# First metric block beside the normalisation, root of the shift bound on VectorE, and closing work spread wider, in an attention layer with a gated feed-forward

## The chip, the cores and the metric

The kernel runs on one core of a Trainium2 chip. The metric is the device time of one execution in microseconds, lower is better. The kernel before takes 607.02 us, the median of three runs (606.62 to 607.74).

## What is computed

One transformer layer on a single sequence of 2048 tokens with 128 features, in fp32. Both halves are gated residuals on a modulated layer norm; the attention works on a hyperbolic log map and multiplies its queries by a learned metric. Cut to what matters:

```python
h = layernorm(x) * (1 + ca) + sa
v = log_map(mu, project(h))            # sqrt, arccosh, one factor for each token
q, k, vv = v @ Wq.T, v @ Wk.T, v @ Wv.T            # 16 heads of width 8
g = |eta + 0.1 * tanh(tanh((h - mu) @ W1.T + b1) @ W2.T + b2)|   # the metric
at = softmax((q * g) @ k.T / sqrt(8))  # 16 heads, 2048 x 2048
x = x + ga * project(mu + 0.1 * (at @ vv) @ Wo.T)
h = layernorm(x) * (1 + cb) + sb
x = x + gb * (silu(h @ wg.T) * (h @ wu.T)) @ wd.T  # hidden width 384
```

## The kernel before

Tokens are cut into four blocks of 512 queries (`NB`, `BT`) and sixteen key tiles of 128 (`NT`). The program has three parts.

*Opening.* VectorE, ScalarE and GpSimd normalise all tokens, and TensorE transposes them (`metric_T`). ScalarE copies the four transposed blocks out (`copy_hT`), then takes the square roots and the logarithm of the log map (`root`, line 433, and line 448), each on request of VectorE, which scales the result to `v` (line 976). Only behind that come the metric of block 0 (`tanh1`, `metric2`, `tanh2`, lines 422 to 431 and 585), the keys of all four blocks (`k_of`), the queries of block 0 (`q_of`), and the splitting of each into three bf16 parts (`k_split1`, `k_rest`, `k_low`, `q_split1`, `queries_rest`, `queries_low`). The parts go to DRAM and come back with another partition layout (`store_k`, `load_k`, `load_q` on SyncE's queue, in written order). The softmax isn't shifted by the true maximum but by a bound: the largest key norm times the query norm of the head. `nk` and `nq` sum the squares, `k_max` takes the maximum, block by block in one PSUM bank, `bound` takes the square root on ScalarE, and `shift` writes the row that `load_shift` puts beside the queries. The first score matmul waits for that row.

*Four blocks* (`block_steps`). A block has 64 steps (`STEPS`): four groups of four heads, each over 16 key tiles. Step j issues on TensorE the scores of two head pairs (`score(j, 0)` and `score(j, 1)`, line 703, sixteen matmuls in all) and between them the product of step j - 2 with the values (`product`, line 720, eight matmuls). ScalarE takes two exponentials of 128x1024 in a step (line 510). Scores lie in three slots of two PSUM banks each, used in turn (`u % 3`); a score waits until the exponential of the slot's last user is done. The count starts anew with each block; since 128 isn't a multiple of three, the first two scores of a block fall on the slots of the last two exponentials before them, and steps 1 and 63 issue their product ahead of the first score. After 16 steps a group's sums are copied out by VectorE (`evacuate`, line 1100), and the next group's first product waits for it (`o_evac`).

In block 0 the steps also carry the values (`V_AT`) and metric, queries and query norms of blocks 1 to 3, at steps written by hand: `M1_AT`, `M2_AT`, `Q_AT`, `NQ_AT`. All of them, as the closing work later, share one PSUM bank (`M_bank`). `nq(b)` puts a block's query norms there, VectorE copies them away (`queries_norm`, line 1065) and signals `nq_sb`, and `metric1(b + 1, 0)` on TensorE, the next to write the bank, waits for `nq_sb` (line 576). After step 49 (`ROOT_AT`) ScalarE takes the three roots (line 473) together.

In blocks 1 to 3 the steps also carry the closing work of the block before, at `AT_WO`, `AT_TR`, `AT_GATE`, `AT_UP` and `AT_DOWN`: output projection, transpose, three gate and three up matmul groups, and the down projection in four pieces.

*The end.* The closing work of block 3 stands alone.

All engines run their own list in order. TensorE's is one list: a wait in it holds all that stands behind.

Of the kernel before, what the change touches and what calls it, by code (L numbers as in the profile page):

```python
# [24 lines left out]
ALU = mybir.AluOpType  # L25
# [31 lines left out]
AT_WO, AT_TR, AT_GATE, AT_UP, AT_DOWN = 8, 15, (19, 24, 29), (22, 27, 32), (37, 39, 41, 43)  # L57
# [3 lines left out]
M1_AT, M2_AT, Q_AT, NQ_AT, ROOT_AT = ((7, 10), (21, 24), (35, 38)), (13, 27, 41), (16, 30, 44), (19, 33, 47), 49  # L61
# [17 lines left out]
def build(nc, x, columns, wmod, fixed, w1t, w2t, w_att, wgt, wut, wdt, out):  # L79
    with ExitStack() as ctx:  # L80
# [27 lines left out]
        hs_bf = sb("hs_bf", [P, H], BF16)  # L108
# [21 lines left out]
        def tmp(words, *shape, dt=F32):  # L130
# [5 lines left out]
            if len(shape) == 2:  # L136
# [10 lines left out]
        shift_f = [O_sb[0:H, 0, :], O_sb[0:H, 3, :], x_res[0:H, :, :].rearrange("p a b -> p (a b)"),  # L147
                   h_tm[0:H, 0:TPB, :].rearrange("p a b -> p (a b)")]
# [58 lines left out]
        names = """c_in wmod_in w_in hs_ready ffn_in const_ready pe_mod mod_ready silu_ready ffn_ready  # L207
# [21 lines left out]
        def ring(j):  # L229

            return j % RING if j < STEPS - 1 else 1
# [137 lines left out]
        def _(pool):  # L369
            pool.memset(half[:, :], 0.5).then_inc(S["const_ready"], 1)  # L370
            pool.memset(mhalf[:, :], -0.5).then_inc(S["const_ready"], 1)
            pool.memset(V_op[:, :, :], 1.0).then_inc(S["ones_ready"], 1)
            pool.wait_ge(S["const_ready"], 2)
# [13 lines left out]
            pool.tensor_copy(hs_bf[:, :], hs_sb).then_inc(S["hs_ready"], 1)  # L387
# [24 lines left out]
        def _(act):  # L412
# [29 lines left out]
            for b in range(NB):  # L442
                copy_hT(b)
# [4 lines left out]
            act.activation(ln_u, u, ACT.Ln).then_inc(S["ln_out"], 1)  # L448

# [5 lines left out]
            def k_split1(b):  # L455
# [3 lines left out]
                act.activation(k_parts[b][:, 0, :], bank(2 + b % 2), ACT.Identity).then_inc(S["k_hi"], 1)  # L459
                act.activation(sqks[b], bank(2 + b % 2), ACT.Square).then_inc(S["k_sq"], 1)  # L460
# [5 lines left out]
            def bound(b):  # L466

                if b == 0:
                    act.wait_ge(S["nq_ps"], 1)
                    act.wait_ge(S["kmax_ready"], 1)  # L470
                else:
                    act.wait_ge(S["nq_sb"], b)
                act.activation(shift_f[b], bank(6)[0:H, :] if b == 0 else shift_f[b], ACT.Sqrt,
                               scale=kmax[0:H, NB:NB + 1]).then_inc(S["bound"], 1)

            for m in range(MH):
                tanh1(0, m)
            copy_vT(0)
            copy_vT(1)
            k_split1(0)  # L480
            tanh2(0)
            act.wait_ge(S["k_res"], 1)
            act.activation(k_parts[0][:, 1, :], rks[0], ACT.Identity).then_inc(S["k_mid"], 1)
            q_split1()
            k_split1(1)
            act.wait_ge(S["q_res"], 1)
            act.activation(q_parts[0][:, 1, :], rqs[0], ACT.Identity).then_inc(S["q_mid"], 1)
            k_split1(2)
            k_split1(3)
            act.activation(sqq[:, :], g_fm[:, 0, :], ACT.Square).then_inc(S["q_sq"], 1)  # L490
            bound(0)
            act.activation(silu_c[:, 1:2], c_c, ACT.Exp).then_inc(S["exp_table"], 1)

            def later(j):
# [9 lines left out]
            def block_steps(Bk, tails):  # L504
                for j in range(STEPS):
                    for half_ in range(2):
# [3 lines left out]
                        act.activation(probs[:, 2 * ring(j) + half_, :], slot_bank(u % 3), ACT.Exp)\  # L510
# [18 lines left out]
            def blocks(p):  # L529
                block_steps(NB * p, False)  # L530
                with act.Fori(NB * p + 1, NB * (p + 1)) as Bk:
                    block_steps(Bk, True)
# [15 lines left out]
        def _(pe):  # L548
# [41 lines left out]
            for b in range(NB):  # L590
                metric_T(b)
            for m in range(MH):
                metric1(0, m)

# [7 lines left out]
            def k_of(b):  # L602
                pe.wait_ge(*((S["vT_sb"], b + 1) if b < 2 else (S["vT_late"], b - 1)))
                if b >= 2:
                    pe.wait_ge(S["k_sq"], b - 1)
                    pe.wait_ge(S["k_res"], b - 1)
                else:
                    pe.wait_ge(S["m1_sb"], MH)
                pe.matmul(bank(2 + b % 2), wk_sb, vT[:, b, :], start=True, stop=True).then_inc(S["k_ps"], 1)  # L609
# [7 lines left out]
            def nk(b):  # L617
                pe.wait_ge(S["k_sq"], b + 1)
                pe.wait_ge(*((S["nk_done"], b) if b else (S["vT_late"], 1)))
                pe.matmul(bank(0)[0:H, :], hs_bf[:, :], sqks[b], start=True, stop=True).then_inc(S["nk_ps"], 1)  # L620
# [10 lines left out]
            def nq(b):  # L631
                pe.wait_ge(S["q_sq"], b + 1)
                pe.wait_ge(S["q_f"], b + 1)
                pe.matmul((M_bank if b else bank(6))[0:H, :], hs_bf[:, :], sqq[:, :], start=True, stop=True)\
# [7 lines left out]

            v_T(0)
            v_T(1)
            k_of(0)
            metric2(0)
            v_T(2)
            v_T(3)
            q_of(0)
            for b in range(1, NB):  # L650
                k_of(b)
            pe.wait_ge(S["hs_ready"], 1)
            for b in range(NB):
                nk(b)
            nq(0)

# [13 lines left out]

            def keep_warm(n, to):

                for _ in range(n):
                    ins = pe.matmul(to, ones_bf[:, 0:P], ones_bf[:, 0:BT], start=True, stop=True)  # L674
                ins.then_inc(S["warm"], 1)


            def score(Bk, j, p, half_):
# [14 lines left out]
                if u >= 3:  # L693
# [3 lines left out]
                for i in range(2):  # L697
                    h = GH * g + 2 * half_ + i
                    if isinstance(Bk, int):
                        at_q = (Bk % 2) * H * BT + h * BT  # L700
                        for c in range(COLS):
                            at_k = P * (kt % TPB) + CW * c
                            ins = pe.matmul(slot_bank(u % 3)[CW * c:CW * (c + 1), i, :],  # L703
                                            K_op[0:rows, kt // TPB, h, at_k:at_k + CW], Q_op[0:rows, at_q:at_q + BT],
                                            start=True, stop=True, tile_position=(0, CW * c))
                    else:
                        ins = pe.matmul(slot_bank(u % 3)[:, i, :],
# [4 lines left out]
            def product(Bk, j):  # L712
# [5 lines left out]
                for i in range(GH):  # L718
                    h = GH * g + i
                    ins = pe.matmul(O_bank[32 * i:32 * (i + 1), :], V_op[:, kt, VW * h:VW * h + 32],  # L720
                                    probs[:, 2 * ring(j) + i // 2, BT * (i % 2):BT * (i % 2 + 1)],
# [37 lines left out]
            def block_steps(Bk, tails, p):  # L759
                for j in range(STEPS):  # L760
                    early = j in (1, STEPS - 1)
                    if not early:
                        score(Bk, j, p, 0)
                    if j >= 2:
                        product(Bk, j - 2)
                    elif tails:
                        product(Bk - 1, STEPS + j - 2)
                    if early:
# [16 lines left out]
            def blocks(p):  # L785
# [16 lines left out]
                product(last, STEPS - 2)  # L802
                product(last, STEPS - 1)
# [27 lines left out]
            keep_warm(7, M_bank)  # L831
            for done, n in (("vT_late", 2), ("k_sq", NB), ("k_res", NB), ("nk_done", NB), ("bound", 1)):
# [24 lines left out]
        def _(dve):  # L857
# [24 lines left out]
            vec.did(dve.memset(flag_f[:, :], 1.0))  # L882

# [60 lines left out]
            dve.tensor_scalar(a2, n2, 1.0, EPS, ALU.add, ALU.add).then_inc(S["root_in"], 1)  # L944
            dve.wait_ge(S["root_out"], 2)
# [35 lines left out]
            def metric(b):  # L981

                vec.after()
                dve.wait_ge(S["m2_sb"], b + 1)
                vec.did(dve.tensor_scalar(g_fm[:, b, :], g_fm[:, b, :], 0.1 * DH ** -0.5, eta_s, ALU.mult, ALU.add))  # L985

# [19 lines left out]
            def k_max(b):  # L1006
                dve.wait_ge(S["nk_ps"], b + 1)
                dve.tensor_reduce(kmax[0:H, b:b + 1], bank(0)[0:H, :], AX.X, ALU.max).then_inc(S["nk_done"], 1)  # L1008

            def shift(b):  # L1010

                dve.wait_ge(S["bound"], b + 1)
# [3 lines left out]
            vec.did(dve.tensor_scalar(eta_s, eta_c, DH ** -0.5, None, ALU.mult))  # L1016
            def k_rest(b):
                dve.wait_ge(S["k_sq"], b + 1)
# [309 lines left out]
```

## Time and profile before

| | us |
|---|---|
| median of three runs | 607.02 |
| profiled execution, device time | 608.64 |
| its span, first to last instruction | 606.6 |
| outside the span | 2.0 |
| TensorE busy (matmul) | 544.9 |
| ScalarE busy | 524.8 |
| VectorE busy | 152.6 |
| GpSimd busy | 21.5 |

Busy time is the union of the instructions' durations; a matmul's duration contains the depth of the pipeline, so the distance of starts tells more than the busy share. "PEclk" is the granted TensorE clock as a share of full speed: 1.00 is 2.4 GHz, 0.50 is 1.2 GHz. In the timeline, rows of the same instruction that follow one another closely are merged: start, time from the first start to the last end, engine, line, operands, count, and in brackets the idle time before and what ended it. In the chain of waits a piece lasts until the next piece of the path begins.

### The profile page before, as it was taken

To read this page: it belongs to the slowest core of one execution; us is meant where nothing else is said; L and a number is where in the kernel's file an instruction comes from. 1 tells how busy PE (TensorE), PEld (TensorE's weight loads), DVE (VectorE), ACT (ScalarE), POOL (GpSimd) and SP (SyncE) were. 2 spreads that over 40 slices of the span, in tenths; PEclk is the share of its full clock that TensorE was granted. 3 is DMA by queue.
4 is the path that set the end of the run, shared out by engine and by line. 5 is a ranking of instruction groups with operands and counts; after the bars stand their busy time and mean duration, and the time that the engine had idled before them with its cause. 6 is when DMAs were issued, how large, how long until landed. Compare 5 with 4: busy or idle time off the path is not lost.

```text
span 606.6 us, 16308 instructions
## 1 busy us (share of the span) xinstructions
PE 544.9 (90%) x7196; PEld 239.8 (40%) x7196; DVE 152.6 (25%) x420; ACT 524.8 (87%) x595; POOL 21.5 (4%) x25
## 2 busy tenths in 40 slices
PE   1466998999979999999999999999999999999544
PEld 0232543554423334455323444554334444543122
DVE  6963303030310361100003611000016211000363
ACT  3564898999999999999999999999999999999401
POOL 2300100000000010000000100000001000000010
PEclk9576999999989999999999999999999999999958
DMA  6012267010030200001002100000000000010000
GB/s 186 3 37 84 91 164 183 3 35 3 28 106 1 70 22 10 3 11 37 10 3 53 37 11 1 11 27 20 2 10 2 11 1 11 2 45 1 1 0 23
DMA packets 13626, 20.64 MB, mean 34 GB/s; under 512 B 2027, under 2 KB 10347, under 8 KB 13267
## 3 DMA queue, kind: packets, MB, share of 16 engines
q1 hardware_dynamic: 12707, 17.22, 11.0%
q0 software_dynamic: 560, 1.97, 0.9%
q8 instruction: 58, 0.95, 0.7%
q10 hardware_dynamic: 288, 0.40, 0.2%
q14 instruction: 13, 0.11, 0.1%
HBM read 13.15 MB, written 4.19 MB: 29 GB/s over the span
## 4 chain that ended last, share of the span: by engine, by line
PE 64%; ACT 15%; DVE 7%; issue 7%; DMA 4%; SPq 1%; POOL 0%; ACTq 0%; DVEq 0%
PE ps L703 27%; PE ps L720 26%; ACT probs L510 13%; PE ps L639 8%; DMA K_op<-k_scr 2%; DVE probs L939 1%; DMA k_scr<-arena 1%; DMA probs<-x_dram 1%; PE ps L674 1%; PE ps L609 1%; DVE arena L1143 1%; ACT arena L440 1%; SPq L262 0%; DVE kmax L1008 0%; PE ps L735 0%
## 5 line engine op out<-in xcount | busy, mean ns | idle before, releaser
L510 ACT ACTIVATE probs<-ps 128x1024 f32<-128x1024 f32 x512 | 481.4, 1116 | 16.9 <-PE ps L703 15.3
L703 PE MATMUL ps<-Q_op,K_op 73*32 73x512 bf16 x4096 | 293.0, 381 | 10.7 <-ACT probs L510 6.7
L720 PE MATMUL ps<-probs,V_op 128*32 128x512 f32 x2048 | 273.1, 595 | 1.2 <-ACT probs L510 0.8
L703 PEld LDWEIGHTS ps<-Q_op,K_op 73*32 73x32 bf16 x4096 | 122.5, 96 | 232.7 <-issue 120.5
L720 PEld LDWEIGHTS ps<-probs,V_op 128*32 128x32 f32 x2048 | 71.3, 110 | 49.3 <-issue 5.4
L1100 DVE COPY O_sb<-ps 128x512 f32<-128x512 f32 x16 | 11.1, 692 | 154.4 <-PE ps L720 154.4
L560 PE MATMUL ps<-fixed_sb,arena 128*128 128x128 f32 x32 | 7.4, 391 | 15.1 <-POOL arena L384 11.1
L1203 DVE SCALAR_TENSOR_TENSOR arena<-arena,ps 128x512 f32<-128x512 f32 x12 | 8.3, 688 | 45.0 <-ACT arena L527 45.0
L522 ACT ACTIVATE arena<-ps 128x512 f32<-128x512 f32 x4 | 2.8, 705 | 18.5 <-PE ps L735 18.5
L1209 DVE TENSOR_TENSOR arena<-ps,arena 128x512 f32<-128x512 f32 x12 | 8.3, 692 | 40.4 <-PE ps L639 40.3
L378 POOL TENSOR_TENSOR small<-small,half 128x4 f32<-128x4 f32 x4 | 4.1, 1014 | 404.6 <-DVE small L1173 404.6
L1221 DVE TENSOR_TENSOR arena<-ps,mod 128x512 f32<-128x512 f32 x3 | 2.1, 692 | 59.9 <-PE ps L639 59.9
L985 DVE TENSOR_SCALAR arena<-arena,cols 128x512 f32<-128x512 f32 x4 | 1.9, 485 | 60.2 <-ACT arena L431 60.2
L639 PE MATMUL ps<-w_att_sb,arena 128*32 128x128 f32 x256 | 10.2, 309 | 5.7 <-DVE arena L1147 5.7
L674 PE MATMUL ps<-ones_bf 128*128 128x512 bf16 x16 | 7.3, 627 | 7.9 <-POOL small L378 7.9
L1143 DVE RECIPROCAL arena<-arena 128x512 f32<-128x512 f32 x4 | 13.4, 3352 | 0.1
L639 PE MATMUL ps<-wd_f,arena 128*32 128x128 f32 x384 | 13.2, 272 | 0.0
L639 PE MATMUL ps<-arena,wg_f 128*32 128x512 f32 x96 | 12.9, 601 | 0.0
L560 PEld LDWEIGHTS ps<-fixed_sb,arena 128*128 128x128 f32 x32 | 5.3, 198 | 18.9 <-issue 8.4
L639 PE MATMUL ps<-arena,wu_f 128*32 128x512 f32 x96 | 12.7, 592 | 0.0
L639 PE MATMUL ps<-Q_op,w_sb 128*32 128x512 f32 x96 | 12.5, 591 | 0.0
L639 PEld LDWEIGHTS ps<-wd_f,arena 128*32 128x32 f32 x384 | 11.6, 109 | 2.3 <-issue 0.6
(162 smaller groups left out, 241.6 us busy)
## 6 DMA issues: line engine op xcount, KB each, us to landing
K_op<-k_scr SPq DMA_DIRECT2D x16, 288.0 KB
Q_op<-q_scr SPq DMA_DIRECT2D x9, 384.0 KB
arena<-O_sb SPq DMA_DIRECT2D x120, 16.0 KB
q_scr<-arena POOLq DMA_DIRECT2D x3, 384.0 KB, 3.0
probs<-x_dram SPq DMA_DIRECT2D x4, 256.0 KB, 5.2
x_res<-x_dram SPq DMA_DIRECT2D x4, 256.0 KB, 3.1
out_dram<-arena SPq DMA_DIRECT2D x4, 256.0 KB, 2.4
Q_op<-q_scr SPq DMA_DIRECT2D x3, 288.0 KB
```

Of the source, the lines that this page charges most:

```text
L440: act.activation(h_tm[:, t, :], x_tm[:, t, :], ACT.Identity, scale=rstd[:, t:t + 1], bias=nmr[:, t:t + 1]).then_inc(S["xn_done"], 1)
L510: act.activation(probs[:, 2 * ring(j) + half_, :], slot_bank(u % 3), ACT.Exp)\
L560: ins = pe.transpose(bank(b % 2)[:, P * t:P * (t + 1)], src[:, TPB * b + t, :], ident_sb)
L609: pe.matmul(bank(2 + b % 2), wk_sb, vT[:, b, :], start=True, stop=True).then_inc(S["k_ps"], 1)
L639: ins = pe.matmul(to[CW * c:CW * (c + 1), :], weights[:, CW * c:CW * (c + 1)], moving, start=start, stop=stop, tile_position=(0, CW * c))
L674: ins = pe.matmul(to, ones_bf[:, 0:P], ones_bf[:, 0:BT], start=True, stop=True)
L703: ins = pe.matmul(slot_bank(u % 3)[CW * c:CW * (c + 1), i, :], K_op[0:rows, kt // TPB, h, at_k:at_k + CW], Q_op[0:rows, at_q:at_q + BT], s ...
L720: ins = pe.matmul(O_bank[32 * i:32 * (i + 1), :], V_op[:, kt, VW * h:VW * h + 32], probs[:, 2 * ring(j) + i // 2, BT * (i % 2):BT * (i % 2 ...
L1100: dve.tensor_copy(O_sb[:, g, :], O_bank).then_inc(S["o_evac"], 1)
L1143: c.did(dve.reciprocal(rec_T, rec_T))
L1203: dve.scalar_tensor_tensor(gl[m], th[m], 1.0, gates, ALU.add, ALU.mult).then_inc(S["gated"], 1)
L1209: dve.tensor_tensor(hid[:, m, :], ups, gl[m], ALU.mult).then_inc(S["glu_done"], 1)
```

## The change

- Opening: the metric of block 0 moves ahead of the roots. TensorE transposes block 0, runs `metric1` twice, then transposes block 1, runs `metric2`, then the other transposes. ScalarE does likewise and takes the roots behind it. Behind the logarithm a square root of a constant is added, so that `bound` finds its table loaded. Ten matmuls without use (`keep_warm`) stand ahead of `v_T(0)`, and ten in place of seven ahead of block 0.
- Each block's keys get a PSUM bank of their own; the four `nk` write 32 rows each of one bank, and one maximum over 128 rows takes the place of four.
- The square roots of blocks 1 to 3 leave ScalarE. `queries_norm` on VectorE takes seven instructions on 16x512: multiply, shift the bits right by one, add a constant, reciprocal, multiply, add, halve. The last one signals `nq_sb`. `shift(b)` follows each.
- The three score slots and the ring of probabilities are counted on from block to block; no step issues its product first. ScalarE's blocks 1 to 3 are written out in place of a loop.
- Closing work: gate, up and down move from (19, 24, 29), (22, 27, 32), (37, 39, 41, 43) to (19, 27, 35), (23, 31, 39), (43, 47, 51, 55); VectorE's second and third `evacuate` move ahead of the last gate and of `result`.

```diff
-AT_WO, AT_TR, AT_GATE, AT_UP, AT_DOWN = 8, 15, (19, 24, 29), (22, 27, 32), (37, 39, 41, 43)
+AT_WO, AT_TR, AT_GATE, AT_UP, AT_DOWN = 8, 15, (19, 27, 35), (23, 31, 39), (43, 47, 51, 55)
...
-M1_AT, M2_AT, Q_AT, NQ_AT, ROOT_AT = ((7, 10), (21, 24), (35, 38)), (13, 27, 41), (16, 30, 44), (19, 33, 47), 49
+M1_AT, M2_AT, Q_AT, NQ_AT = ((7, 10), (21, 24), (35, 38)), (13, 27, 41), (16, 30, 44), (19, 33, 47)
...
+        def slot(Bk, p, u):
+
+            return (u + 2 * STEPS * Bk) % 3 if p == 0 else u % 3
+
+        def early(p, j):
+
+            return p == 1 and j in (1, STEPS - 1)
...
-            for b in range(NB):
-                copy_hT(b)
+            copy_hT(0)
+            for m in range(MH):
+                tanh1(0, m)
+            copy_hT(1)
+            tanh2(0)
+            copy_hT(2)
+            copy_hT(3)
             root(y0, a2, 2)
             root(rt, t2, 3)
             root(dn, inn, 4)
             act.wait_ge(S["ln_in"], 1)
             act.activation(ln_u, u, ACT.Ln).then_inc(S["ln_out"], 1)
+            act.wait_ge(S["const_ready"], 2)
+            act.activation(kmax[:, 7:8], half[:, 0:1], ACT.Sqrt)
...
-                    if j == ROOT_AT:
-                        bound(b)
...
-                if u >= 3:
+                if u >= 3 or (p == 0 and not start):
                     pe.wait_ge(S["exped"], Bk * 2 * STEPS + u - 2)
...
+            keep_warm(10, bank(5))
             v_T(0)
             v_T(1)
             k_of(0)
-            metric2(0)
+            q_of(0)
...
             def queries_norm(b):
                 dve.wait_ge(S["nq_ps"], b + 1)
-                dve.tensor_copy(shift_f[b], M_bank[0:H, :]).then_inc(S["nq_sb"], 1)
-
+                vec.did(dve.tensor_scalar(root_a, M_bank[0:H, :], kmax[0:H, NB:NB + 1], None, ALU.mult))
+                vec.after()
+                vec.did(dve.tensor_scalar(root_b.bitcast(I32), root_a.bitcast(I32), 1, None,
+                                          ALU.logical_shift_right))
+                vec.after()
+                vec.did(dve.tensor_scalar(root_b.bitcast(I32), root_b.bitcast(I32), 0x1FBD0000, None,
+                                          ALU.add))
+                vec.after()
+                vec.did(dve.reciprocal(shift_f[b], root_b))
+                vec.after()
+                vec.did(dve.tensor_tensor(shift_f[b], shift_f[b], root_a, ALU.mult))
+                vec.after()
+                vec.did(dve.tensor_tensor(root_b, shift_f[b], root_b, ALU.add))
+                vec.after()
+                dve.tensor_scalar(shift_f[b], root_b, 0.5, None, ALU.mult).then_inc(S["nq_sb"], 1)
...
                 if b == 2:
                     evacuate(0, 1)
                 queries_norm(b)
+                shift(b)
             evacuate(0, 2)
-            for b in range(1, NB):
-                shift(b)
```

## Rows read from the trace of the kernel before

**Rows 1.** Busy time by stretch: start and end, length, engines' busy time, granted clock, DMA
```profile
315.50:439.00 123.50, 122.54 (x1724) 53.14 (x1720) 22.69 (x52) 121.14 (x134) 2.01 (x2) 1.00 0.08 20
```

**Rows 2.** Timeline of ScalarE, around the end of block 2
```profile
411.76 24.90 ACT L510 ACTIVATE probs<-ps 128x1024 f32<-128x1024 f32 x27
...
435.27 8.73 ACT L510 ACTIVATE probs<-ps 128x1024 f32<-128x1024 f32 x9
...
445.56 1.94 ACT L510 ACTIVATE probs<-ps 128x1024 f32<-128x1024 f32 x2 [0.27 <-PE ps L703]
```

**Rows 3.** Chain of waits in block 2: start, length, piece
```profile
366.37 0.86 PE ps L639 x8
...
368.52 0.86 PE ps L703 x16
369.38 0.86 PE ps L720 x8
```

**Rows 4.** Timeline of ScalarE in block 2, where the down projection runs
```profile
399.01 3.84 ACT L510 ACTIVATE probs<-ps 128x1024 f32<-128x1024 f32 x4 [0.27 <-PE ps L703]
403.12 3.84 ACT L510 ACTIVATE probs<-ps 128x1024 f32<-128x1024 f32 x4 [0.27 <-PE ps L703]
```

**Rows 5.** Timeline of ScalarE in block 0, from before the three roots
```profile
151.91 12.93 ACT L510 ACTIVATE probs<-ps 128x1024 f32<-128x1024 f32 x14
164.87 1.28 ACT L473 ACT_TABLE_LOAD   x1
...
169.42 4.69 ACT L510 ACTIVATE probs<-ps 128x1024 f32<-128x1024 f32 x5
175.00 7.44 ACT L510 ACTIVATE probs<-ps 128x1024 f32<-128x1024 f32 x8 [0.89 <-PE ps L703]
```

**Rows 6.** Timeline of VectorE: two query norms, an evacuation, a reciprocal and its neighbours
```profile
102.71 0.68 DVE L1065 COPY O_sb<-ps 16x512 f32<-16x512 f32 x1 [1.33 <-PE ps L634]
...
160.08 0.68 DVE L1065 COPY arena<-ps 16x512 f32<-16x512 f32 x1 [1.52 <-PE ps L634]
163.15 0.69 DVE L1100 COPY O_sb<-ps 128x512 f32<-128x512 f32 x1 [2.39 <-PE ps L720]
...
329.19 0.43 DVE L1141 TENSOR_SCALAR arena<-arena 128x512 f32<-128x512 f32 x1 [6.80 <-DMA arena<-O_sb]
329.65 3.35 DVE L1143 RECIPROCAL arena<-arena 128x512 f32<-128x512 f32 x1
...
333.04 0.69 DVE L1147 TENSOR_TENSOR arena<-arena 128x512 f32<-128x512 f32 x1
```

**Rows 7.** Timeline of TensorE in block 0: a metric matmul, a product, a restart
```profile
105.78 1.21 PE L639 MATMUL ps<-Q_op,w_sb 128*32 128x512 f32 x8
...
163.99 1.07 PE L720 MATMUL ps<-probs,V_op 128*32 128x512 f32 x8
...
170.49 0.61 PE L703 MATMUL ps<-Q_op,K_op 73*32 73x512 bf16 x8 [3.71 <-ACT probs L510]
```

**Rows 8.** Busy time by stretch, with granted clock behind TensorE's restart
```profile
171.40:174.70 3.30, 3.29 (x24) 0.98 (x28) 0.00 (x0) 2.71 (x3) 0.00 (x0) 0.50 0.63 159
```

**Rows 9.** Timeline of the opening: first copy, first root, TensorE's restart, loads, first scores
```profile
19.26 0.67 ACT L420 ACTIVATE Q_op<-ps,cols 128x512 f32<-128x512 f32 x1
...
27.26 0.21 ACT L435 ACTIVATE small<-small 128x16 f32<-128x16 f32 x1 [0.49 <-DVE small L944]
...
32.77 1.97 PE L560 MATMUL ps<-fixed_sb,arena 128*128 128x128 f32 x8 [3.99 <-DVE arena L976]
...
36.44 2.77 PE L585 MATMUL ps<-Q_op,w_sb 128*128 128x512 f32 x4
...
48.30 2.06 SPq L269 DMA_DIRECT2D Q_op<-q_scr  x3
...
55.41 0.60 SPq L278 DMA_DIRECT2D Q_op<-wmod_sb  x1
...
57.70 1.05 PE L703 MATMUL ps<-Q_op,K_op 73*32 73x512 bf16 x16 [2.24 <-DMA Q_op<-wmod_sb]
```

More of the change, by code:

```diff
@@ L464, in q_split1, with bound @@
                 act.activation(q_parts[0][:, 0, :], g_fm[:, 0, :], ACT.Identity).then_inc(S["q_hi"], 1)
[L466 to L473, printed above, removed]
+            def bound():
+                act.wait_ge(S["nq_ps"], 1)
+                act.wait_ge(S["kmax_ready"], 1)
+                act.activation(shift_f[0], bank(6)[0:H, :], ACT.Sqrt,
                                scale=kmax[0:H, NB:NB + 1]).then_inc(S["bound"], 1)
-            for m in range(MH):
-                tanh1(0, m)
             copy_vT(0)
             copy_vT(1)
-            k_split1(0)
-            tanh2(0)
+            k_square(0)
+            k_high(0)
+            copy_vT(2)
+            k_square(1)
+            q_split1()
             act.wait_ge(S["k_res"], 1)
             act.activation(k_parts[0][:, 1, :], rks[0], ACT.Identity).then_inc(S["k_mid"], 1)
-            q_split1()
-            k_split1(1)
+            k_square(2)
             act.wait_ge(S["q_res"], 1)
             act.activation(q_parts[0][:, 1, :], rqs[0], ACT.Identity).then_inc(S["q_mid"], 1)
-            k_split1(2)
-            k_split1(3)
             act.activation(sqq[:, :], g_fm[:, 0, :], ACT.Square).then_inc(S["q_sq"], 1)
-            bound(0)
+            k_square(3)
+            k_high(1)
+            bound()
             act.activation(silu_c[:, 1:2], c_c, ACT.Exp).then_inc(S["exp_table"], 1)
+            k_high(2)
+            k_high(3)
             def later(j):
@@ L529, in blocks @@
             def blocks(p):
-                block_steps(NB * p, False)
-                with act.Fori(NB * p + 1, NB * (p + 1)) as Bk:
-                    block_steps(Bk, True)
+                block_steps(NB * p, False, p)
+                if p == 0:
+                    for Bk in range(1, NB):
+                        block_steps(Bk, True, p)
+                else:
+                    with act.Fori(NB * p + 1, NB * (p + 1)) as Bk:
+                        block_steps(Bk, True, p)
                 last = NB * (p + 1) - 1
@@ L588, in metric2 @@
                 ins.then_inc(S["m2_ps"], 1)
-            for b in range(NB):
-                metric_T(b)
+            metric_T(0)
             for m in range(MH):
                 metric1(0, m)
+            metric_T(1)
+            metric2(0)
+            metric_T(2)
+            metric_T(3)
             def v_T(b):
@@ L602, in k_of @@
             def k_of(b):
[L603 to L609, printed above, removed]
+                pe.wait_ge(*((S["vT_sb"], b + 1) if b < 3 else (S["vT_late"], 1)))
+                pe.wait_ge(S["m1_sb"], MH)
+                pe.matmul(bank(2 + b), wk_sb, vT[:, b, :], start=True, stop=True).then_inc(S["k_ps"], 1)
             def v_of(b):
@@ L641, in by_columns, with keep_warm @@
                 return ins
+            def keep_warm(n, to):
+                for _ in range(n):
+                    ins = pe.matmul(to, ones_bf[:, 0:P], ones_bf[:, 0:BT], start=True, stop=True)
+                ins.then_inc(S["warm"], 1)
+            keep_warm(10, bank(5))
             v_T(0)
@@ L645, in _ @@
             k_of(0)
-            metric2(0)
+            q_of(0)
             v_T(2)
+            k_of(1)
             v_T(3)
-            q_of(0)
-            for b in range(1, NB):
-                k_of(b)
+            k_of(2)
             pe.wait_ge(S["hs_ready"], 1)
-            for b in range(NB):
-                nk(b)
+            pe.wait_ge(S["zero_ready"], 1)
+            nk(0)
+            k_of(3)
+            nk(1)
+            nk(2)
             nq(0)
+            nk(3)
             def later(j):
@@ L669, in later @@
                         nq(b)
[L671 to L675, printed above, removed]
             def score(Bk, j, p, half_):
@@ L801, in blocks @@
                         block_steps(Bk, True, p)
-                product(last, STEPS - 2)
-                product(last, STEPS - 1)
+                product(last, p, STEPS - 2)
+                product(last, p, STEPS - 1)
                 pe.wait_ge(S["o_evac"], NG * (last + 1))
```

116 lines of the change are left out of this document (61 added, 55 removed).

## The prediction

> **What bounds the kernel now.** I read the busy time by stretch first. In blocks 1 to 3 TensorE and ScalarE are both busy nearly throughout: 122.54 and 121.14 of 123.50 us [rows 1]. So neither share names a bound, and the distance of starts has to. Next the timeline of ScalarE where nothing is inserted: from 411.76 to 435.27 lie 26 exponentials, 0.904 us each, 1.81 a step [rows 2]. TensorE's side comes from the chain of waits: sixteen score matmuls 0.86, eight of the product 0.86, so 1.725 a step, and a gate or up group adds 0.86 [rows 3]. ScalarE sets the pace in plain steps and TensorE catches up 0.085 a step; where work is inserted TensorE sets it. At the down pieces four exponentials take 4.11 us (399.01 to 403.12) in place of 3.62 [rows 4]. Whatever stops TensorE for longer than the half microsecond or so that the slots cover reaches ScalarE in full. That decides this change: the question for each edit is whether TensorE is stopped.
>
> **Base.** The profiled execution took 608.64 us, its span 606.6 and 2.0 around it. That is 1.6 above the median of 607.02. I sum differences and put them on the median, since only differences are forecast.
>
> **Block boundaries: -3.7.** From 435.27 to 445.56 stand ten distances of exponentials (one more lies between the two rows); ten plain ones would take 9.04, so 1.25 is lost to the slots' restart and the two steps with the product first [rows 2]. The end of block 1 shows the same and the end of block 0 0.2 less; three make 3.6 to 3.7. Counted on, a boundary is a plain step. What is late next there is the product behind the fourth evacuation; inside a block the same wait stands at each group's end without a loss in ScalarE's pace. Bounds: nothing to 3.7.
>
> **Closing work wider: -2.5.** The stretch bound by TensorE ran from step 19 to 43 and now runs to 55. Twelve more steps go at 1.725 in place of 1.81: 1.0 a block. Against it, the evacuation at step 49 now falls in that stretch. At a group's end the product waits for a copy of 0.69 [rows 6] that the scores beside it (0.86) nearly cover, so 0.2. That leaves 0.8, times three. `result` ends some twelve steps later; on SyncE's queue the store, the reload of x and one gather stand behind it, and they still end before the block does, at nothing. Were that cover gone, the next `normalise` would start later, ahead of `AT_WO` by several steps, still at nothing. Bounds: 0 to 4.
>
> **ScalarE's roots leave block 0: -5.9.** Fourteen exponentials from 151.91 should be followed by the next at 164.57; it comes at 169.42, 4.85 later. Five further on, 175.00 stands where 173.94 was due, 1.06 more: TensorE restarted after 3.71 idle and ran at half clock from 171.4 to 174.7 [rows 5, 7, 8]. Both go.
>
> **What VectorE's roots add in block 0: +12.1.** This is the largest term, and it hides in one semaphore. Before, `nq_sb` came with a copy of 0.68, at 102.71 + 0.68 [rows 6]; now it comes with the seventh instruction. Prices on 512 elements: a multiply from PSUM 0.68; shift and add of a constant, SBUF to SBUF, 0.46 apart as 329.19 to 329.65; reciprocal 3.39 as 329.65 to 333.04; two tensor by tensor at 0.69 and 0.04 between; halving 0.43 [rows 6]. Sum: 0.72 + 0.46 + 0.46 + 3.39 + 0.73 + 0.73 + 0.43 = 6.92. No row shows a reciprocal on 16 partitions, but the copy takes 0.68 on 16 and 0.69 on 128 [rows 6], so width doesn't count. No row shows the integer shift and add; between 0.3 and 0.7 each I take 0.46, the row of the same form.
> Who waits: `metric1(2, 0)` at step 21 on TensorE started at 105.78 without a wait [rows 7]. The signal now comes at 102.71 + 6.92 = 109.63, and 0.15 on TensorE starts (as from 163.84, the evacuation's end, to 163.99): it stands for 4.0. The pattern stands twice (step 35 for block 3, 0.2 less): 7.8. The third chain starts at 160.08, with `shift` (0.45) ends at 167.45, and only then comes `evacuate(0, 2)`, which started at 163.15 before [rows 6]. The product at 163.99 [rows 7] moves by 4.3. All three stop TensorE where it is already level with ScalarE (an insertion of 0.86 at steps 21 and 35, the evacuation at 50), so they count in full.
> The Trainium skill's page "VectorE: DVE Perf Modes", section on mode 2x_2P, says that an operation with one tensor source, both sides in SBUF, takes two elements a cycle whatever its width. The trace agrees for fp32 (0.43 against 0.69 with two sources) and shows no integer one. Without that mode for the shift and the add, at 0.69 each, the chain would be 7.4 and the term 13.5.
>
> **The clock behind these stops: +4.8.** After 3.71 idle TensorE had 3.3 us or more at half clock [rows 7, 8], that is some 1.7 us of work lost, of which ScalarE felt 1.06 with all slots full. The three new stops are 4.0, 3.8 and 4.7 long and leave the slots empty, so I take 1.6 each. Bounds: 0.5 each if the stretch falls partly into the stop, 2.7 each if a second one follows.
>
> **Opening: -2.2.** The log map's first root runs at 27.26, as soon as VectorE asks [rows 9]. Now there stand ahead of it in ScalarE's order two `tanh1`, `tanh2`, two more copies and two table loads of 1.28 [rows 5]; between them, in series, two `metric1` and `metric2` of 2.8 us or more at half clock [rows 9], 1.9 at full. From the first copy's end at 19.9 [rows 9]: 3.9 for `metric1`, 0.7, then `metric2` 2.0 (3.7 at half clock), 0.7, two copies 1.3, load 1.3. The root comes at 29.7 (31.5), so 2.4 to 4.5 late, and all of the log map with it. TensorE restarts at 35.2 in place of 32.77. The ten extra matmuls end well before and hide there; since TensorE idles several us behind them I give them no clock.
> Behind the restart `metric2`, three of four maxima and the table load ahead of `bound` go, which would bring the shift row about 8 us forward. But SyncE's order binds then: from the restart to `load_q` 15.5 (48.30), its issue 2.06, and the last load's 2.29 (55.41 to 57.70) make 19.9 in place of 24.9 [rows 9]. `load_q` waits for the splits of q, whose order is hardly changed. First scores at 55.1, 2.6 earlier; 0.4 off for a cold start after a longer stop. Bounds: -3 to 0.
> The Trainium skill's page "ScalarE: Activation LUTs", section "What ACT_TABLE_LOAD costs", adds a drain of 1.38 to each switch of tables. The trace disagrees: two loads and three roots fit in 4.85 [rows 5]. By the page the opening would lose some 1.4 more.
>
> **Sum.** -3.7 - 2.5 - 5.9 + 12.1 + 4.8 - 2.2 = +2.6, so 609.6.
>
> **Rivals.**
> (a) Slower still: two half-clock stretches behind each stop (+3) and the opening at its bad end (+2): 614. For it: each stop is longer than the one that cost 3.3 us at half clock. 0.18.
> (b) About the same: the clock costs 0.5 each (-3.3) and the opening gives 2.6: 605.9. For it: a stretch at half clock can lie inside the stop. 0.19.
> (c) Faster, the other side: the root chain is short. It decides at 3.07 us, the time from 160.08 to 163.15 [rows 6]; below it no stop is left, and without 12.1 and 4.8 the time is 592.7. It would need a reciprocal that costs less on 16 partitions. Against it: the copy's two widths. 0.08.
> (d) The boundary doesn't become a plain step, because the product behind the evacuation stops TensorE at a new block's start: 613.3. 0.07.
> (e) The page's drain holds here: 611. 0.03.
>
> **How the numbers follow.** The forecast, 608.2 to 612, has 0.45. About 0.2%, 1.2 us, is what a measurement of this kernel can tell from no change. Slower by more (above 608.2): forecast, (a), (d), (e), 0.72 rounded. Within: most of (b), 0.15. Faster: (c) and the rest of (b), 0.13. The range 604.8 to 613.6 leaves out (c), and about half of (a).
>
> **What would show it.** Right: in block 0 two idle times of TensorE near 4 us that end with VectorE's seventh root instruction, at steps 21 and 35, one near 4.7 before the product of step 50, each with clock 0.50 behind; exponentials 0.904 apart across block ends; first root near 29.7, first scores near 55. Wrong: a reciprocal far below 3.35, or gaps of ScalarE there below 3 us.

## The result, and the profile after

The changed kernel takes 613.87 us (median of four runs, 612.88 to 616.57), the kernel before 606.82 beside it: ratio 1.0109, 95% interval 1.0079 to 1.0139. On the 607.02 that the forecast stood on that is 613.6, or +6.6 us [+4.8, +8.4] where +2.6 was forecast: slower, as forecast, but above the forecast's own band of 608.2 to 612 and at the upper end of its range, 604.8 to 613.6. The profiled execution took 614.84, its span 613.0.

From the page of the changed kernel: busy times, TensorE's clock by slice, and two of the costliest groups (line, engine, operands, count, busy, mean ns, idle before and what ended most of it):

```profile
PE 547.3 (89%) x7209; PEld 242.1 (39%) x7209; DVE 168.2 (27%) x437; ACT 520.3 (85%) x593; POOL 21.6 (4%) x26
PEclk9777999898989999999999999999999999999958
L662 PE MATMUL ps<-Q_op,w_sb 128*32 128x512 f32 x96 | 13.3, 644 | 7.2 <-DVE O_sb L1112 7.2
L746 PE MATMUL ps<-probs,V_op 128*32 128x512 f32 x2048 | 273.8, 600 | 5.5 <-DVE O_sb L1140 4.5
```

ScalarE is busy 4.5 us less than before and VectorE 15.6 more, neither of which is the loss. It is in the last two rows: TensorE idles 7.2 us ahead of `metric1`, always for line 1112, the last of the seven root instructions, and 4.5 ahead of products for an evacuation. The clock's digits are for slices of 15.3 us: 9 from the thirteenth to the 58 of the last part, so blocks 1 to 3 are undisturbed. The three 8s are slices 8, 10 and 12, 107 to 123, 138 to 153 and 169 to 184 us, all in block 0; there lie the stops.

The timeline of block 0, in three excerpts: the chain at step 21 with what waits for it, the second stop, and the third at step 50. Rows of other engines that lie between are left out.

```profile
102.17 0.74 DVE L1098 TENSOR_SCALAR x_res<-ps,kmax 16x512 f32<-16x512 f32 x1 [1.33 <-PE ps L657]
102.95 0.42 DVE L1100 TENSOR_SCALAR arena<-x_res 16x512 int32<-16x512 int32 x1
103.40 0.41 DVE L1103 TENSOR_SCALAR arena<-arena 16x512 int32<-16x512 int32 x1
103.85 3.34 DVE L1106 RECIPROCAL O_sb<-arena 16x512 f32<-16x512 f32 x1
107.22 0.68 DVE L1108 TENSOR_TENSOR O_sb<-O_sb,x_res 16x512 f32<-16x512 f32 x1
107.94 0.68 DVE L1110 TENSOR_TENSOR arena<-O_sb,arena 16x512 f32<-16x512 f32 x1
108.65 0.41 DVE L1112 TENSOR_SCALAR O_sb<-arena 16x512 f32<-16x512 f32 x1
109.21 1.63 PE L662 MATMUL ps<-Q_op,w_sb 128*32 128x512 f32 x8 [3.62 <-DVE O_sb L1112]
111.73 1.02 ACT L529 ACTIVATE probs<-ps 128x1024 f32<-128x1024 f32 x1 [4.93 <-PE ps L729]
...
143.37 1.66 PE L662 MATMUL ps<-Q_op,w_sb 128*32 128x512 f32 x8 [3.57 <-DVE O_sb L1112]
...
170.49 0.74 DVE L1098 TENSOR_SCALAR x_res<-ps,kmax 16x512 f32<-16x512 f32 x1 [1.53 <-PE ps L657]
...
177.76 0.67 DVE L1140 COPY O_sb<-ps 128x512 f32<-128x512 f32 x1
178.58 1.94 PE L746 MATMUL ps<-probs,V_op 128*32 128x512 f32 x8 [4.24 <-DVE O_sb L1140]
181.41 1.94 ACT L529 ACTIVATE probs<-ps 128x1024 f32<-128x1024 f32 x2 [5.23 <-PE ps L729]
184.82 5.61 ACT L529 ACTIVATE probs<-ps 128x1024 f32<-128x1024 f32 x6 [1.48 <-PE ps L729]
```

From 102.17 to TensorE's restart are 7.04 us; the chain of rows 6 with the start behind it had been priced at 7.07. And busy time by stretch, columns as in rows 1 (the granted clock is the third number from the end): the three stretches behind the stops, and one of block 2.

```profile
109.60:113.00 3.40, 3.40 (x24) 1.30 (x20) 0.00 (x0) 1.02 (x1) 0.00 (x0) 0.50 0.00 0
143.70:147.10 3.40, 3.40 (x24) 1.27 (x20) 0.00 (x0) 1.02 (x1) 0.00 (x0) 0.50 0.00 0
177.90:184.60 6.70, 6.02 (x44) 2.15 (x48) 1.42 (x6) 1.94 (x2) 0.00 (x0) 0.50 0.24 59
315.50:439.00 123.50, 123.41 (x1748) 54.46 (x1744) 22.67 (x52) 122.12 (x135) 2.02 (x2) 1.00 0.09 22
```

Each stop is followed by TensorE at 1.2 GHz, for 3.4 us twice and for 6.7 the third time. The last row answers rows 1: ScalarE has 135 instructions in the same 123.50 us for 134.

To price each place I took the distances between exponentials a step apart and summed what each exceeds 1.81 by. At steps 21 and 22 the excess is 5.08 and 1.68 (before: 0.29 and 0.97), at 35 and 36 5.06 and 1.65 (0.28, 0.98), at 50 and 51 5.49 and 1.60 (nothing). The new part is 5.5 + 5.45 + 7.1 = 18.0. The old stall of the three roots, 5.87, is gone. Net +12.2 in this execution, where the prediction's three terms (12.1 + 4.8 - 5.9) had 11.0.

### The profile page after: what moved, and what is told of

It is laid out like the page before. It is cut to its first block, busy times and chain, and to the rows that moved or that the text cites. A ratio compares the mean times of both kernels' runs of the same rounds, so it can differ in the third digit from the quotient of the medians.

```text
span 613.0 us, 15951 instructions
## 1 busy us (share of the span) xinstructions
PE 547.3 (89%) x7209; PEld 242.1 (39%) x7209; DVE 168.2 (27%) x437; ACT 520.3 (85%) x593; POOL 21.6 (4%) x26
## 3 DMA queue, kind: packets, MB, share of 16 engines
q1 hardware_dynamic: 12707, 17.22, 10.9%
## 4 chain that ended last, share of the span: by engine, by line
PE 79%; DVE 8%; DMA 5%; ACT 4%; SPq 1%; issue 1%; POOL 0%; DVEq 0%
PE ps L729 34%; PE ps L746 33%; PE ps L662 8%; DMA K_op<-k_scr 2%; ACT probs L529 2%; DVE O_sb L1106 2%; ACT arena L452 1%; DMA k_scr<-arena 1%; DMA probs<-x_dram 1%; PE ps L583 1%; PE ps L669 1%; SPq L280 1%; SPq L273 1%; PE ps L595 1%; DVE arena L1182 1%
## 5 line engine op out<-in xcount | busy, mean ns | idle before, releaser
L729 PE MATMUL ps<-Q_op,K_op 73*32 73x512 bf16 x4096 | 290.0, 383 | 8.2 <-DMA Q_op<-wmod_sb 6.9
L729 PEld LDWEIGHTS ps<-Q_op,K_op 73*32 73x32 bf16 x4096 | 124.4, 96 | 229.2 <-issue 136.7
L669 PE MATMUL ps<-ones_bf 128*128 128x512 bf16 x29 | 8.9, 457 | 7.9 <-POOL small L390 7.9
L662 PEld LDWEIGHTS ps<-w_att_sb,arena 128*32 128x32 f32 x256 | 8.5, 126 | 8.6 <-DVE arena L1186 6.6
```

Of the source, the lines that this page charges most:

```text
L662: ins = pe.matmul(to[CW * c:CW * (c + 1), :], weights[:, CW * c:CW * (c + 1)], moving, start=start, stop=stop, tile_position=(0, CW * c))
L729: ins = pe.matmul(slot_bank(slot(Bk, p, u))[CW * c:CW * (c + 1), i, :], K_op[0:rows, kt // TPB, h, at_k:at_k + CW], Q_op[0:rows, at_q:at_q ...
```

## The experiments

All kernels named here compute the whole output. Ratios are to the kernel before, run on the same chip.

**The bank's release and the place of the evacuation.** My theory: the stops come from what the last root instruction signals, and from the evacuation queued behind the third chain; not from VectorE's work. The rival: the 6.9 us of root work that VectorE has three times in block 0 delays something whatever the signal is. The first kernel lets the multiply, the only instruction that reads the bank, signal `nq_sb`; the second puts the evacuation ahead of the third chain; the third does both. `shift`, which had waited for `nq_sb`, now waits for the last root instruction.

```diff
-                vec.did(dve.tensor_scalar(root_a, M_bank[0:H, :], kmax[0:H, NB:NB + 1], None, ALU.mult))
-                vec.after()
+                dve.tensor_scalar(root_a, M_bank[0:H, :], kmax[0:H, NB:NB + 1], None, ALU.mult).then_inc(S["nq_sb"], 1)
+                dve.wait_ge(S["nq_sb"], b)
...
-                dve.tensor_scalar(shift_f[b], root_b, 0.5, None, ALU.mult).then_inc(S["nq_sb"], 1)
+                vec.did(dve.tensor_scalar(shift_f[b], root_b, 0.5, None, ALU.mult))
```
```diff
-                if b == 2:
-                    evacuate(0, 1)
+                if b >= 2:
+                    evacuate(0, b - 1)
                 queries_norm(b)
                 shift(b)
-            evacuate(0, 2)
```

> The changed kernel, with one edit: nq_sb is signalled by the first of the seven root instructions, the only one that reads the shared PSUM bank. Theory (the late signal holds TensorE at steps 21 and 35): both waits of 3.6 us in the trace vanish and with them the half-clock stretches behind them, 5.5 us of ScalarE's time each, so 11 us less than the changed kernel: ratio to before 0.993 (about 603). The stop before the product of step 50 stays, 7.1 us. Rival (VectorE's 7 us of root work delays whatever comes next on it, wherever the signal stands): less than 3 us come back, ratio above 1.006.

> The changed kernel, with the third evacuation ahead of the root chain of block 3 on VectorE. Theory: the product of step 50 finds its bank free, the stop of 4.2 us and the two half-clock stretches behind it go, 7.1 us of ScalarE's time: ratio to before 1.000 (about 607). The two stops at steps 21 and 35 stay. Rival (the third root chain must end before something else that is just as late, the query load of block 1 above all, which waits for two shift rows): the time moves to that wait, less than 2 us come back.

> Both edits. Theory: no TensorE stop above 1 us is left in block 0, 18 us less than the changed kernel, ratio to before 0.982 (about 596). Rival: the stops share a cause and less than the sum comes back.

Measured: 0.9886 [0.9841, 0.9931], 1.0000 [0.9968, 1.0033] and 0.980 [0.9755, 0.9844], medians 601.75, 608.42 and 596.61. From the changed kernel the steps are -13.5, -6.6 and, both together, -18.8 us. The first gave more than the 11 expected; in its trace block 0 is 10.9 shorter than in the changed kernel's, and its exponentials also begin 1.3 earlier, where it has no edit. In the third kernel's trace the chain runs just as long (timeline, TensorE at step 21 and VectorE around step 49):

```profile
105.19 1.21 PE L662 MATMUL ps<-Q_op,w_sb 128*32 128x512 f32 x8
...
162.56 0.69 DVE L1143 COPY O_sb<-ps 128x512 f32<-128x512 f32 x1 [4.59 <-PE ps L746]
163.17 0.73 DVE L1101 TENSOR_SCALAR x_res<-ps,kmax 16x512 f32<-16x512 f32 x1
...
164.84 3.34 DVE L1109 RECIPROCAL O_sb<-arena 16x512 f32<-16x512 f32 x1
```

Neither `metric1` at steps 21 and 35 nor the product of step 50 has an idle time there, and the distances of the exponentials at steps 21, 22, 35 and 36 are those of the kernel before again, at 50 and 51 plain ones. The rival falls: the same arithmetic on VectorE costs nothing that the trace shows once nobody waits for it. The changed kernel lost its time to a signal and to a place in a queue.

**The later roots back on ScalarE.** Everything else of the change stays; the old `queries_norm`, `bound(b)` and `ROOT_AT` return. That tells what the rest of the change is worth.

```diff
+                    if j == ROOT_AT:
+                        bound(b)
...
+                dve.tensor_copy(shift_f[b], M_bank[0:H, :]).then_inc(S["nq_sb"], 1)
```

> The changed kernel with the three later roots back on ScalarE after step 49, as before the change; opening, slots and closing work stay changed. Theory: the three stops (18.0 us of ScalarE's time) go and the old one (5.9 us) returns, 12.1 us less: ratio 0.991 (about 601.8). That is the sum of all other parts against before: -5.2. Rival (the other parts hold part of the loss): above 605.

Measured 0.9926 [0.9898, 0.9953], 602.59 us. So the rest gives -4.5 us, and the roots on VectorE in the changed kernel's form cost 1.0109 - 0.9926 = 0.0183, some 11.1 us (by the two intervals, 2.5 either way). The forecast had 11.0 for the same three terms, as worked out above.

**The parts one at a time, put into the kernel before.** Slots and ring counted on, with ScalarE's blocks written out; then the closing work spread with its evacuations; then the opening.

```diff
+            return (u + 2 * STEPS * Bk) % 3 if p == 0 else u % 3
...
+            return p == 1 and j in (1, STEPS - 1)
```
```diff
-AT_WO, AT_TR, AT_GATE, AT_UP, AT_DOWN = 8, 15, (19, 24, 29), (22, 27, 32), (37, 39, 41, 43)
+AT_WO, AT_TR, AT_GATE, AT_UP, AT_DOWN = 8, 15, (19, 27, 35), (23, 31, 39), (43, 47, 51, 55)
```
```diff
-            for b in range(NB):
-                copy_hT(b)
+            copy_hT(0)
+            for m in range(MH):
+                tanh1(0, m)
+            copy_hT(1)
+            tanh2(0)
+            copy_hT(2)
+            copy_hT(3)
```

> The kernel before with the slot and ring counting alone (and ScalarE's blocks 1 to 3 written out). Prediction: three boundaries become plain steps, -3.6 us, ratio 0.994. From the changed kernel's trace: steps 62, 63 and 0 at 1.81 us. Rival (the boundary's wait moves to the product behind the evacuation): nearer to 1.000.

> The kernel before with the wider closing work and its two evacuations alone. Prediction: 0.8 us in each of three blocks, -2.5 us, ratio 0.996. Rival (the evacuation of step 49 and the output projection of step 8 collide with the late pieces): at most half of it.

> The kernel before with the opening alone (first metric ahead of the roots, a bank for each key block, one maximum, matmuls without use). Forecast of the record -2.2 us; the changed kernel's trace shows the first exponential 0.3 us earlier than before, so -0.3 us and a ratio of 0.9995. Rival (the opening's gain is there but eaten by a cold start of the scores): the first exponential earlier by more than 1 us in this run, and steps 0 and 1 longer.

Measured 0.9953 [0.993, 0.9976], 0.9961 [0.994, 0.9982] and 1.0018 [0.9995, 1.0041]: -2.9, -2.4 and +1.1 us. Their sum, -4.2, agrees with the -4.5 of the kernel with the roots on ScalarE, so the parts add up as far as the intervals (1.3 to 1.4 us each way) can tell. The rival of the third falls: its first exponential starts at 58.16, 0.2 and not over 1 us earlier than in the profile before. The boundary behind block 2 in the changed kernel, and the down pieces there, on ScalarE's timeline:

```profile
406.86 22.65 ACT L529 ACTIVATE probs<-ps 128x1024 f32<-128x1024 f32 x24 [0.27 <-PE ps L729]
...
439.16 22.11 ACT L529 ACTIVATE probs<-ps 128x1024 f32<-128x1024 f32 x24
```

Block 3 begins at 450.92, in the middle of the second row (24 exponentials from 439.16 on): no break stands there, where rows 2 have three rows for it. And 24 exponentials stand together where rows 4 have a break after each four. The 22.65 has room for 23 distances of 0.94, with TensorE's insertions in it, against the 4.11 for four (1.03 each) of the denser schedule.

**The clock behind the stops.** The changed kernel, with matmuls without use ahead of the three waits (17, 17 and 19 of them, written to a part of the bank that nobody reads), so that TensorE still waits as long but isn't idle. The rival: half clock behind a stop costs little, since ScalarE's pace would be the limit after it anyway.

```diff
+                    pe.matmul(M_bank[96:128, :], ones_bf[:, 0:CW], ones_bf[:, 0:BT], start=True, stop=True,
+                              tile_position=(0, 96))
...
+                    if b >= 2:
+                        fill(17)
...
+                    if isinstance(Bk, int) and Bk == 0 and g == 3:
+                        fill(19)
```

> The changed kernel with 17 matmuls without use ahead of each of TensorE's two waits for nq_sb and 19 ahead of the wait of step 50, written to 32 rows of the shared bank that nobody reads then. The waits stay, but TensorE is busy in them. It tells the wait from the clock behind it. Forecast: waits of 3.6, 3.6 and 4.2 us as they are, no stretch at 0.50 behind them; the clock's share of the loss was 1.5 each behind the first two and 2.8 behind the third in the changed kernel, so 5 us less, ratio to before 1.003. Rival (the price behind the stops is the refilling of the slots, not the clock): the same time as the changed kernel, ratio 1.011.

Measured 0.9991 [0.9961, 1.002], 606.78 us: 0.0118 under the changed kernel, 7.2 us (2.6 either way), where 5 was expected; the rival, no gain, falls. Its timeline on TensorE at the first stop, and the stretches behind the first and the third:

```profile
103.39 3.83 PE L595 MATMUL ps<-ones_bf 128*32 128x512 bf16 x17
107.25 1.06 PE L670 MATMUL ps<-Q_op,w_sb 128*32 128x512 f32 x8
```
```profile
107.30:110.70 3.40, 3.40 (x44) 1.32 (x48) 0.35 (x1) 1.64 (x2) 0.00 (x0) 1.00 0.00 0
...
173.10:180.00 6.90, 6.90 (x96) 2.91 (x100) 0.83 (x5) 5.36 (x6) 0.00 (x0) 1.00 0.24 61
```

`metric1` waits for the same signal, and behind it the clock is 1.00 with 44 matmul records in 3.40 us, where the changed kernel has 24. This splits the stops. The waits alone leave 3.71, 3.70 and 4.14 above the old pace, 11.55 together; what vanished is the clock's part, 18.0 - 11.55 = 6.5 in the traces.

**What holds the opening.** The changed kernel's trace, in which SyncE's issues (SPq) carry the answer; ahead of them the first root on ScalarE and TensorE's restart:

```profile
29.52 0.21 ACT L447 ACTIVATE small<-small 128x16 f32<-128x16 f32 x1
...
35.03 1.97 PE L583 MATMUL ps<-fixed_sb,arena 128*128 128x128 f32 x8 [5.67 <-DVE arena L1011]
...
46.45 0.43 SPq L294 DMA_DIRECT2D q_scr<-arena  x1
47.80 0.83 SPq L273 DMA_DIRECT2D K_op<-k_scr  x1
48.68 0.98 SPq L294 DMA_DIRECT2D q_scr<-arena  x2
52.45 2.06 SPq L280 DMA_DIRECT2D Q_op<-q_scr  x3
54.56 0.60 SPq L289 DMA_DIRECT2D Q_op<-wmod_sb  x1
...
56.99 1.90 PE L729 MATMUL ps<-Q_op,K_op 73*32 73x512 bf16 x16 [6.95 <-DMA Q_op<-wmod_sb]
```

The second and third stores of q stand behind the wait for the keys' stores; the load of q waits for all three. My theory: that order costs about the time from the first to the last q store. The rival: q's split parts are the limit and the order is harmless. The kernel is the third above with the three stores ahead of the wait:

```diff
-                if n == 0:
-                    sp.wait_ge(k_st[0], 16 * PARTS)
-                    load_k(0, 0, K_first[0])
+            sp.wait_ge(k_st[0], 16 * PARTS)
+            load_k(0, 0, K_first[0])
             sp.wait_ge(q_st[0], 16 * PARTS)
```

> The kernel of both edits, with SyncE's queue reordered: the stores of the second and third query part stand ahead of the wait for the stored keys and the key load of block 0. Theory of the opening (the query load at 52.45 waits for query parts that were ready at 47.06 but stood behind the key load's wait): the query load starts some 2.4 us earlier and the first scores 2 us earlier, so 594.5 against 596.6, ratio 0.977. Rival (the key load comes later by as much, or the clock is the limit): the same time as without.

Measured 0.977 [0.9733, 0.9807], 593.02 us; the third kernel had 0.980. The medians differ by 3.6 us, the ratios by 1.8, and the intervals overlap, so the gain rests on the trace as well:

```profile
46.27 1.41 SPq L294 DMA_DIRECT2D q_scr<-arena  x3
47.72 0.83 SPq L273 DMA_DIRECT2D K_op<-k_scr  x1
49.07 2.04 SPq L280 DMA_DIRECT2D Q_op<-q_scr  x3
51.16 0.60 SPq L289 DMA_DIRECT2D Q_op<-wmod_sb  x1
```

Against the third kernel (load of q at 52.54, keys' load at 47.82, shift row at 54.65), the load of q goes out 3.5 us earlier, the keys' load not a bit later, and the shift row 3.5 earlier; the first exponential starts at 55.08 in place of 58.26. The last part of q was ready at 46.87, and at 47.06 in the changed kernel: the parts came at nearly the same time and the load moved by 3.5, so the rival falls.

**The metric moved back off the log map's path, and the ten matmuls.** The first of these two takes the kernel just shown and leaves only block 0's first half of the metric ahead of the roots (`tanh2` and `metric2` go behind the logarithm and the other transposes, the square root of the constant to just ahead of `bound`). The second leaves out the ten matmuls ahead of `v_T(0)`.

```diff
-            copy_hT(1)
-            tanh2(0)
-            copy_hT(2)
-            copy_hT(3)
+            for b in range(1, NB):
+                copy_hT(b)
...
+            tanh2(0)
```
```diff
-            keep_warm(10, bank(5))
             v_T(0)
```

> The reordered-queue kernel with tanh2 and metric2 of block 0 behind the other transposes and behind the logarithm, so that ScalarE takes the first root after two tanh1 and four copies. Theory (the opening's loss is the work ahead of the first root): the first root near 27.8 in place of 29.5, the first scores up to 1.7 us earlier, ratio 0.974. Rival (tanh2 with its table load now delays the copies of v and the queries instead): no gain.

> The reordered-queue kernel without the ten matmuls ahead of v_T(0). TensorE idles 5.7 us behind them, so no clock is bought and none lost: same time, ratio 0.977. Rival (they shift the grant so that the keys run at full clock): 1 us slower, and a longer stretch at 0.50 behind the restart near 35 us.

Measured 0.974 [0.9684, 0.9797] and 0.9755 [0.9705, 0.9805], 592.51 and 593.37 us. Neither can be told from 0.977. The first did what it was built for and got nothing for it. Its first root, and TensorE at step 15, with the piece from the chain of waits that ends there (start, length, piece):

```profile
28.43 0.22 ACT L446 ACTIVATE small<-small 128x16 f32<-128x16 f32 x1
```
```profile
90.42 0.62 PE L726 MATMUL ps<-Q_op,K_op 73*32 73x512 bf16 x8 [1.69 <-DMA K_op<-k_scr]
```
```profile
76.68 13.70 DMA K_op<-k_scr
```

The first exponential starts at 53.76, 1.3 earlier than in the kernel it came from. At step 15 the scores then wait for the load of later keys, 13.70 us from issue to landing, and steps 0 and 1 take 0.9 more. Block 0 takes 2.9 longer altogether and ends 1.5 later. In the kernel without the ten matmuls the same piece lasts 14.63. This wait isn't new: at the same step the kernel before has 1.74 us of it and the changed kernel 1.23. Nor does it follow the start alone: the kernel with the stores first starts at 55.08 and has none, the one without the ten matmuls starts at 56.05 and has 2.77. A start that is further forward can lose there what it gained; how often it does, one trace a kernel can't tell.

As for the ten matmuls: without them the half-clock stretch around TensorE's restart lasts from 31.4 to 41.6, with them from 34.1 to 40.9. Most of the difference lies where TensorE has nothing to do, but the stretch also ends 0.7 later, and the first exponential starts 1.0 later (56.05 for 55.08). The profiled execution without them took 598.01, the slowest of its five. No difference in time can be measured, and the rival, 1 us, is within the intervals: it stays open.

## Why the prediction was right in its kind and too small

**The base and the bound.** Right: blocks 1 to 3 are undisturbed, and every stop of TensorE over half a microsecond in block 0 reached ScalarE.

**Boundaries (-3.7 forecast, -2.9 measured).** Right in the mechanism: steps 62, 63 and 0 are plain now, as the rows above show. What the term left out: of the 3.6 that they gave, part comes back at steps 2 and 8 of the next block, up to 0.09 and 0.41 in the kernel with this part alone (1.2 over three blocks) and 0.28, 0.15 and 0.15 at step 8 in the changed kernel, while before step 8 showed nothing. The two medians can't tell -2.9 from -3.7. I haven't found what step 8 waits for; a plausible reading is that TensorE catches up 0.085 a step from a boundary on and has less in hand at `AT_WO`, but no run tests it.

**Closing work wider (-2.5 forecast, -2.4 measured).** Right; in the trace of this part alone a good 1.0 a block, where 0.8 was forecast.

**ScalarE's roots leave (-5.9) and the root chain stops TensorE (+12.1).** Right in every step: who signals, who waits, the order of the evacuation, the length of the chain. The stops of the waits alone are 11.55 for 12.1. A reciprocal on 16 partitions takes 3.34, on 128 it took 3.35 [rows 6], so width doesn't count, and rival (c), which needed a cheap one, is refuted by the row itself. The integer shift and add take 0.42 and 0.41, against 0.43 for the fp32 form [rows 6]. Here the trace agrees with the Trainium skill's page "VectorE: DVE Perf Modes", section on mode 2x_2P, that the fast mode holds whatever the width is; the 13.5 worked out for the other case has no ground.

**The clock behind the stops (+4.8 forecast, 6.5 in the traces and 7.2 in the medians).** Mis-sized. The first two stops cost 1.8 each for 1.6, which is as forecast. The third cost 3.0: two half-clock stretches followed it, 6.7 us together. That was rival (a) for one stop of three. In the kernel with the early release alone the same product stops for 4.23, and only 3.4 us behind it ran at half clock; so the second stretch isn't a matter of the stop's length. Nor is it this kernel's alone: the old stop of the roots, 3.7 us long in five traces, was followed by 3.4 us at half clock in the kernel before and in the one with the closing work alone, and by 6.8 in the one with the later roots on ScalarE and in those with the slots and the opening alone. So the 1.06 of rows 5, from which the 1.6 was taken, was the cheaper of two outcomes: in these three the steps behind the stop lose 1.8 to 2.1. What decides between them stays open.

**Opening (-2.2 forecast, +1.1 measured, -0.3 to +2.5).** This is the step that failed: a gain was forecast, and none is there. The beginning of it is right: first root 29.52 for 29.7, restart 35.03 for 35.2. The first scores come at 56.99 for 55.1. Wrong is "from the restart to `load_q` 15.5": it is 17.4. I had copied the distance of rows 9 and noted that the order of the splits is hardly changed. But the keys' third part ends 11.0 behind the restart in place of 9.2, and on SyncE two stores of q stand behind the wait for the keys' stores. They stood there before the change too, but then q's last part was ready only at 45.52, behind the keys' load at 43.69; now it is ready at 47.06 and the keys' load goes out at 47.80. SyncE's queue should have been walked through. The run with the three stores first shows what it was worth, 3.5 us of `load_q`. What delays the keys' third part no run separates. The 0.4 taken off for a cold start is there: the first exponential follows the first scores by 1.10, by 0.66 in rows 9.

There is a second reason, in the base. The profiled execution of before ran its opening with a mean clock of 0.67 where two other kernels with the same opening had 1.00, and its first exponential stands at 58.36, theirs at 56.27 and 56.26. SyncE's loads in the kernel with the closing work alone, for rows 9:

```profile
47.49 2.06 SPq L269 DMA_DIRECT2D Q_op<-q_scr  x3
...
52.88 0.60 SPq L278 DMA_DIRECT2D Q_op<-wmod_sb  x1
```

The shift row goes out at 52.88 there, at 55.41 in rows 9. So the gain of 2.6 in first scores was measured from an execution 2.1 later than the others. The kernel with the opening alone starts its exponentials at 58.16 and ends block 0 at 196.26, the one with the closing work alone at 194.85: 1.4 later, in line with the +1.1. One profile of the opening is good to some 2 us; the comparison has to be of medians.

**The sum.** Between forecast and result lie 4.0. The opening gave 3.3 of it, the clock 1.7 to 2.4 and the boundaries 0.8, the waits -0.55; these make some 5.5, and the 1.5 too much is within the intervals of the ratios. Rivals: (a) came closest, 614 for 613.6 (its own terms, +3 and +2 on 609.6, make 614.6), with the mechanism right in part: a second stretch behind one stop of three, not behind each, and an opening at or beyond its bad end. (d) named 613.3 for another reason, which the boundary rows refute. (b) needed a clock cost of 0.5 a stop; it was 1.8 and more. (e), the drain at each switch of tables from the Trainium skill's page "ScalarE: Activation LUTs", section "What ACT_TABLE_LOAD costs", has this case against it once more: in the changed kernel's opening the loads take 1.28 each and the next activation starts at once, here ahead of the first root:

```profile
28.23 1.28 ACT L447 ACT_TABLE_LOAD   x1
```

The next instruction is the 29.52 shown above.

## What to carry to other kernels

When a short copy becomes a chain, let the first instruction that frees the shared buffer carry the signal, not the last one that has the result, and put a short operation for which the busiest engine waits ahead of the chain: here these two edits turned +6.6 us into -12.1. Price each stop of TensorE with the clock behind it, here 1.1 to 3.0 us for a stop of 3.6 to 4.2. And when work is moved, walk the new order through every queue, those of the DMAs too, before a distance of the old trace is used again.

## What the runs showed of the hardware

- A stop of TensorE of 3.6 to 4.2 us was followed by 3.4 us at half clock in some traces and by 6.7 to 6.8 in others, for the same stop of 3.7 us too; keeping it busy with matmuls without use during three waits held the clock at 1.00 and gave 7.2 us back, without shortening the waits.
- VectorE's reciprocal takes 3.34 us for 512 elements on 16 partitions as on 128; it is half of the root chain. On integers, shift and add by a constant take 0.42 and 0.41.
- A load of keys of 288 KB, issued beside others, took 13.7 and 14.6 us from issue to landing in two kernels; the scores of step 15 waited 1.69 and 2.77 for it.
- The same opening began its exponentials 2.1 us apart in the executions of two kernels, with the mean clock of 32.8 to 41 us at 0.67 and at 1.00.
